# First layer of a four-layer attention kernel: the same steps, written in another sequence on each of the four compute engines

## The reference, cut to what matters

```python
x = _L0_xattn_ref(x, ctx_2048, mask, ...)       # grouped-query cross attention: the layer that is changed
x = _L1_xattn_ref(ctx_2048, x, ...)             # 16-head cross attention and an MLP
x = _L2_xattn_ref(x, ctx_2048, ...)             # single-head cross attention
x = _L3_xattn_ref(x, ctx_2048, ctx_2048, ...)   # two 16-head cross attentions and an MLP

# layer 0: batch 8, 256 query rows, 64 context rows, width 256, 32 query heads over 8 key heads of 8
q = hidden_state @ Wq + bq
k = encoder_hidden_state @ Wk + bk
v = encoder_hidden_state @ Wv + bv
attn = softmax(q k^T / sqrt(8) + mask)
x = (attn v) @ Wo + bo + hidden_state
return (x - mean(x)) * rsqrt(var(x) + EPS) * gamma + beta
```

## Time and profile before

| | us |
|---|---|
| runs of the kernel | 1105.26, 1107.76, 1110.13 (median 1107.76) |
| the profiled execution | 1105.58, its span 1103.8 |
| PE busy | 1013.5 (92%) |
| DVE busy | 732.4 (66%) |
| ACT busy | 624.9 (57%) |
| POOL busy | 503.4 (46%) |

### The profile page before, as it was taken

One profiled execution on the slowest core, in us unless ns is written; L12 is line 12 of the kernel. 1 busy time (PEld: TensorE's weight loads), 2 busy tenths in 40 slices (PEclk: granted clock), 3 DMA queues, 4 the chain that ended last, 5 costly groups with the idle time before them and its releaser, 6 DMA issues.

```text
span 1103.8 us, 18788 instructions
## 1 busy us (share of the span) xinstructions
PE 1013.5 (92%) x6628; PEld 765.2 (69%) x6628; DVE 732.4 (66%) x1518; ACT 624.9 (57%) x1138; POOL 503.4 (46%) x456
## 2 busy tenths in 40 slices
PE   6887879799999889999999989999999999889998
PEld 3666665466655556777688857887888678767887
DVE  5878775566677461455588876774889677764553
ACT  3777874466666663566378734443787444346543
POOL 3878775533330041112144446764444267646341
PEclk9999999999999999999999999999999999989999
DMA  9010013633332200200022300000331200000000
GB/s 301 12 31 2 1 35 100 178 95 94 95 99 62 78 28 11 68 1 20 20 79 95 106 1 1 1 1 1 96 97 58 77 1 1 1 1 1 20 29 29
DMA packets 37154, 55.97 MB, mean 51 GB/s; under 512 B 12550, under 2 KB 29510, under 8 KB 34758
## 3 DMA queue, kind: packets, MB, share of 16 engines
q1 hardware_dynamic: 34998, 54.25, 16.1%
q10 hardware_dynamic: 2064, 0.52, 0.2%
HBM read 45.34 MB, written 9.18 MB: 49 GB/s over the span
## 4 chain that ended last, share of the span: by engine, by line
PE 70%; DVE 8%; issue 6%; POOL 5%; ACT 5%; SPq 2%; DMA 2%; ACTq 0%; DVEq 0%; POOLq 0%
PE ps L918 8%; PE ps L1216 8%; PE ps L1092 8%; PE ps L988 5%; PE ps L1191 5%; PE ps L1103 4%; PE ps L1113 4%; PE ps L869 4%; PE ps L836 3%; PE ps L767 3%; PE ps L989 3%; PE ps L850 2%; ACT pT L1260 2%; ACT p L1263 1%; SPq L589 1%
## 5 line engine op out<-in xcount | busy, mean ns | idle before, releaser
L1814 DVE TENSOR_REDUCE nm<-ps 128x1 f32<-128x320 f32 x256 | 114.3, 486 | 54.7 <-PE ps L836 52.5
L1260 ACT ACTIVATE pT<-ps 128x512 f32<-128x512 f32 (+1 forms) x144 | 73.9, 563 | 119.2 <-PE ps L1207 90.7
L1216 PE MATMUL ps<-v,pT 128*128 128x256 f32 x512 | 120.4, 389 | 8.7 <-DVE xr L2095 5.6
L2336 POOL TENSOR_TENSOR wl<-bun_m,wh 128x512 fp32r<-128x512 f32 x64 | 80.5, 1262 | 100.3 <-ACT wh L1260 100.3
L1216 PEld LDWEIGHTS ps<-v,pT 128*128 128x128 f32 x512 | 95.8, 192 | 27.8 <-ACT pT L1260 10.5
L2395 POOL TENSOR_TENSOR pn<-p,sm 128x1024 f32<-128x1024 f32 x32 | 60.9, 1903 | 99.0 <-DVE sm L2084 99.0
L988 PE MATMUL ps<-wb,hid_high 128*128 128x512 f32 x256 | 96.8, 415 | 0.0
L1263 ACT ACTIVATE pT<-ps 128x512 f32<-128x512 f32 x160 | 85.3, 607 | 15.9 <-PE ps L850 15.7
L1263 ACT ACTIVATE p<-p 128x1024 f32<-128x1024 f32 (+1 forms) x64 | 68.5, 1071 | 44.9 <-DVE p L2076 42.4
L1191 PE MATMUL ps<-gs,hs 128*128 128x512 f32 x288 | 77.3, 420 | 3.1 <-DVE hs L2089 3.1
L836 PE MATMUL ps<-ks,qs 97*128 97x320 bf16 x256 | 69.4, 305 | 10.6 <-DVE nm L1814 6.3
(11 more groups left out here) (242 smaller groups left out, 2686.9 us busy)
## 6 DMA issues: line engine op xcount, KB each, us to landing
bun_m<-in_heads SPq DMA_DIRECT2D x32, 515.0 KB, 3.5
ks<-k_parts SPq DMA_DIRECT2D x48, 160.0 KB
qs<-q_parts SPq DMA_DIRECT2D x48, 128.0 KB
q_parts<-qp SPq DMA_DIRECT2D x8, 384.0 KB, 3.3
k_parts<-kp SPq DMA_DIRECT2D x8, 384.0 KB, 3.4
w<-in_w SPq DMA_DIRECT2D x2, 1024.0 KB, 4.8
xr<-in_x SPq DMA_DIRECT2D x1, 2048.0 KB, 15.9
out<-xr SPq DMA_DIRECT2D x16, 128.0 KB, 1.7
```

The source lines that it names most:

```text
L1216: last = mm(o, pT3[half][:, n, :], v3[:, bass.ds(i, 1), 4 * half + n, :], start=half == 0 and n == 0, stop=half == 1 and n == 3)
L1260: return nc.scalar.activation(o, x, ACT.Identity, bias=bias, scale=scale)
L1814: v.tensor_reduce(nm1[i % 2][:, t, h:h + 1], ps[:, u % 2, 0:KEYS1], X, ALU.max, negate=True).then_inc(D1t["maxima"].sem, 1)
L2336: g.tensor_tensor(wl3[m % 2][:, cols], bun[m % BUNS][:, cols], wh3[m % 2][:, cols].bitcast(F32), ALU.subtract).then_inc(GH["low"].sem, 1)
```

## The change

Each of the four sequences of layer 0 is written in another order. POOL's special sequence for the last turn (the second string) changes as well. No step, operation, shape, buffer or transfer is added or removed.

```diff
-            for step, i, k in steps0("T1 N-2 S2 V1 H-1 P-1 B0 B1 T2 S3 V2 N-1 T3 H0 V3 P0 T4 Q2 B2 V4 B3"):
+            for step, i, k in steps0("T1 N-2 S2 V1 H-1 P-1 B0 T2 B1 V2 S3 N-1 T3 B2 H0 V3 P0 T4 Q2 B3 V4"):
...
-            for step, i, k in steps0("Q1 O0 R-2 C1 N-2 H-1 O1 E2 C2 R-1 E3 O2 N-1 C3 H0 E4 O3 E5 C4"):
+            for step, i, k in steps0("Q1 O0 R-2 C1 N-2 H-1 E2 O1 C2 E3 R-1 O2 N-1 C3 H0 E4 O3 C4 E5"):
...
-            for step, i, k in steps0("N-2 Q1 H-1 A2 M4 Y-1 H0 N-1 M5 A3 M6 Y0 M7"):
+            for step, i, k in steps0("N-2 Q1 H-1 A2 Y-1 H0 N-1 M4 M5 A3 Y0 M6 M7"):
...
-            for step, i, k in steps0("R-2 G-4 K1 M2 X0 G-3 M3 R-1 M4 M5 X1", "M2 R-2 G-4 M3 X0 G-3 R-1 M4 M5 X1"):
+            for step, i, k in steps0("K1 R-2 G-4 M2 M3 G-3 R-1 X0 X1 M4 M5", "R-2 G-4 M2 X0 X1 M3 G-3 R-1"):
```

## The result

| | before | changed |
|---|---|---|
| median, us | 1107.72 (6 runs, 1105.26 to 1110.13) | 1101.49 (6 runs, 1101.11 to 1103.04) |
| profiled execution | 1105.58, span 1103.8 | 1102.69, span 1100.9 |
| first scores of layer 1 (L836) | 174.30 | 170.76 |

The ratio is 0.9947, with a 95% interval of 0.9932 to 0.9963: 6.2 us less by the medians, where 9.1 was forecast. The two profiled executions show less, 2.9, since that of before lies 2.1 under its median and that of the changed kernel 1.2 above. The traces are therefore read up to the first scores of layer 1 (L836): what follows it took from 928.5 to 931.9 in the traced executions of this study, the same code each time. Up to there the gain is 174.30 - 170.76 = 3.54, where 9.1 was forecast. The missing 5.6 are what has to be explained.

The account below looks back on a forecast made before the run. Layer 0's turns were taken as bound by a loop of waits through all engines, no engine full. Turn 0 -0.2, turns 1 and 2 -5.0, turns 3 to 5 -4.2, turns 6 and 7 +0.3: -9.1, so 1098.7 us, range 1093 to 1107.

Parts of the forecast that it names:

- The full turn: Regular turn of layer 0, `S2` to `S2`: DVE's work, gaps and new waits give 16.2 against 17.6, 1.4 less.
- the loop: Layer 0's circle of waits through all engines, 17.63 a turn; `K`, `G` and `R` on POOL were to leave it.
- the placing by hand: Full turn's steps placed as offsets from `S2` by profiled durations, starting with DVE's `A2` at 3.30 and `Y-1` next.
- its own signs: Listed checks: turn near 16.2, `K` three before `S2`, scores near 165.2; wrong if DVE waits over 1.5 ahead of `Y-1`.
- I assume that this goes with the idle time before it: Turn 2: PE's slow clock was to vanish with the idle time before it, giving 16.2 instead of 20.9.
- Turn 1: POOL's extra work behind `K` makes `R-2` end at 15.9 and `N-2` 1.15 late: 17.35 instead of 17.64.
- its waits come out nearly as before: Turn 0, which has no `Y-1`, `N-1` or `G`: nearly unchanged waits, taken as -0.2.
- Turns 6 and 7: Last two turns up to layer 1's first scores: 36.95 against 36.65, so +0.3, with a POOL wait setting the end.
- the forecast's chain: Last two turns: `X1` 24.2 at best, `R-1` 30.0, `N-1` 30.8, `P0` 33.65, layer 1's first scores 36.95.
- The loads are hidden: Last two turns: stores and loads behind `parts1` end at 35.9, before the scores at 36.95, so they cost nothing.
- The rule on the shared port: Last turns: POOL's `M2` holds the first operation of `parts1` for 1.35, loads land at 37.2, sum -8.9 instead of -9.1.
- a stretch of 0.44: Kernel before: POOL's addition beside `parts1` took 1.17 instead of 0.73; by this reading the loads stay hidden, sum -9.1.

Follow-up runs that it names:

- The single strings: Four kernels, each the kernel before with only one engine's new order (POOL, DVE, ACT or PE): 1102.55, 1110.05, 1101.44 and 1106.34 us.
- e2_filler: Changed kernel with the second half of PE's transposes of unit 1 of batch 2 done three times (added work, same result): 1098.42 us.
- e12_fill7: Changed kernel with the second half of PE's transposes of unit 1 done three times in turns 2 and 7: 1098.52 us.
- e4_own1: Changed kernel with layer 1's first queries' copy on ACT and keys' projection on PE moved one step later: 1101.64 us.
- e6_dve_only: Kernel before with DVE's string of the change alone: 1110.05 us.
- e1_ctx_m2: Changed kernel with POOL's extra work on the context keys directly ahead of `M2` instead of directly behind `K`: 1100.87 us.
- e10_all: Changed kernel with context keys ahead of `M2`, `pc` behind unit 0's exponential, layer 1's queries and keys later, `X1` last on POOL: 1095.19 us, ratio 0.9889 to before.
- e3_last_string: Changed kernel with `X1` moved behind `R-1` in POOL's last turn, instead of ahead of `M3`, `G-3` and `R-1`: 1103.10 us.
- e9_same: Changed kernel once more, unedited: 1102.94 us.
- e11_no_dve: Changed kernel with DVE's string alone put back as it was: 1102.68 us.
- e7_act_only: Kernel before with ACT's string of the change alone: 1101.44 us.
- e8_pe_only: Kernel before with PE's string of the change alone: 1106.34 us.
- e5_pool_only: Kernel before with POOL's two strings of the change alone: 1102.55 us.

## Why the prediction was right about the turn and wrong about its sum

- **The full turn was right**, 16.20 for 16.2, by its own steps: the waits, `K` three before `S2`, `E3` before `R`, `P0` at 10.0. Turns 3 to 5 gave 4.30 for 4.2. The single strings show that the cause was right only in part: `K`, `G` and `R` leaving the loop (POOL's string, 0.78) and `E3` ahead of `R` (ACT's, 0.43) carry it. DVE's own order, with which the placing by hand began, gives 0.07.
- **By its own signs** the forecast failed outside the full turn: layer 1's first scores came at 170.76 and not near 165.2, and in turn 2 DVE waited 2.06 ahead of `Y-1`, over the 1.5 that it named. That the medians still moved by 6.2 is in part luck: 2.7 of it lie outside the 3.54 that the traces show up to L836, in nothing that the forecast describes.
- **Turn 2: the step that failed most** is "I assume that this goes with the idle time before it", the clock at 1.00. The order itself takes 16.2 there (e2_filler, e12_fill7, e4_own1). The slow stretch cost 2.66, the largest part of the missing 5.6. The idle time didn't go: it moved to `N-2` ahead of turn 2, 1.60. And clock and idle time are tied less closely than assumed: in e6_dve_only PE stands idle for the same 1.83 in turn 2 as in the kernel before, and its clock stays at 1.00 there:

```profile
73.33 0.44 PE L743 MATMUL ps<-cst,xn 128*128 128x128 f32 x2 [1.83 <-ACT xn L1260]
...
76.00:80.00 4.00, 3.79 (x35) 3.22 (x36) 3.02 (x7) 3.82 (x8) 2.90 (x4) 1.00 0.00 0
```

- **Turn 1** was put at 17.35 and took 17.69. `R-2` ends at 15.86 after `S2`, forecast 15.9; missed was that ACT's `R` also waits for `G-4` behind it, 0.34.
- **Turn 0** was put at -0.2 ("its waits come out nearly as before") and cost +0.89: 1.09 off. I had looked at what the turn lacks, and not at what hangs on the moved steps: `R-2` behind the second third of the context keys, and `pc` behind `E5`, with `T2`, `B1` and `H0` after it. Moving the keys brings 0.50 (14.86, e1_ctx_m2), moving `pc` as well another 1.14 (13.72, e10_all).
- **Turns 6 and 7** were put at 36.95 and took 38.23, 1.28 off, of which 0.95 is the clock (to half a us). At full clock (e12_fill7) the forecast's chain is there step by step, from `S2` at 129.13: `X1` at 24.3 (forecast 24.2), `R-1` done at 30.25 (30.0), `N-1` at 31.2 (30.8), `P0` at 34.1 (33.65), the scores at 37.28 (36.95). In the changed kernel itself the slow projection comes last instead. The loads are hidden, as forecast.
- 0.28 is the start of turn 0, which lies between 31.28 and 32.63 in the other traces (33.11 in e4_own1, where the clock fell there). The parts sum to 0.28 + 1.09 + 0.34 + 2.66 - 0.10 + 1.28 = 5.55.
- **The rule on the shared port.** The first operation of `parts1` (148.17) took 1.52 beside POOL's `M2`, which ended at 147.24 + 1.90 = 149.14; the same operation took 0.69 with POOL idle (151.66). Held until 149.14 it would have ended at 149.83, and it ended at 149.69. By that rule of the Trainium skill ("SBUF — State Buffer", Who interferes with whom) the two exclude each other for the whole instruction, and the trace agrees to 0.14. The row of before that the prediction read as a stretch of 0.44 fits as well: held until 154.21 + 1.71 = 155.92, POOL's addition would have ended 0.73 later, at 156.65, and it ended at 156.50. The hold cost 0.83 where 1.35 was worked out, since DVE reached it 0.93 after the start of `M2` instead of 0.55, and the loads were hidden all the same.

**What stays open.** The traces account for 3.54 up to L836, the medians for 6.2. The traced execution of before is a short one, where the other runs of before reach to 1110.13 and 1111.04, and no trace shows where those lose time. Of nine later runs of before, the four longest (1108.59 to 1111.04) have a mean granted clock of 0.982 or 0.983, the five others 0.984 to 0.989, so the clock may be part of it. And why the clock of the last two turns stayed at 1.00 in e10_all, which has idle times of PE like the changed kernel's, was not tried apart. The filler's effect rests on few traces: with it turn 2 was clean in two of two, without it, in the same order, in one of four.

## What to carry to other kernels

When an order written by hand is judged by its regular turn, price the first and the last turns separately: walk through what hangs on each moved step there, the extra work of other layers above all. Here the regular turns gave 4.3 as forecast and four small repairs of the irregular ones gave 6.3 more. A reorder that moves an idle time of PE to another place moves the risk of a slow clock with it. And repairs of one stretch don't add up: in the last two turns the slow projection, the chain behind `X1` and the transfer stood close behind one another, and with one gone the next set the time.

## What the hardware showed that I had not expected

- Up to L836 PE's granted clock fell to 0.50 for 3 to 10 us at a time (3.4 in the kernel before, some 6 in the changed one, 10.2 in e6_dve_only), with a price of 2.66 where the loop of waits goes through PE and 0.95 where other waits cover it. The fall depends on the order but isn't fixed by it: with the changed strings of PE, ACT and POOL, the context keys in their old place and no filler, turn 2 was slow in four traces (the changed kernel, e3_last_string, e9_same, e11_no_dve) and clean in one, e4_own1, which fell in turn 0 instead. With the filler it was clean in two of two, and the kernel was quicker with more matmuls in it.
- An idle time of PE was there ahead of the falls, but it doesn't decide alone. The same idle time of 1.2 ahead of an `N` stands in the last two turns of 13 of the 14 traces; the clock fell behind it in nine and stayed at 1.00 in four (before, e7_act_only, e8_pe_only, e10_all). In or just ahead of turn 2 it stayed at 1.00 behind 1.83 (e6_dve_only), 1.60 (e4_own1) and 1.16 (e5_pool_only). What else decides is not shown.
- `parts1` on DVE takes 5.37 with POOL idle for most of it and 8.14 with POOL at work beside it (e3_last_string), the same six operations. A step moved into the wait of one engine can take the gain out of the other.
